# Key/value weight halves side by side in one stationary, and the norms' squares as the moving side of four column-tiled products

## The reference, cut to what matters

```python
qkv = einsum('bsd,ed->bse', x, Wqkv_w) + Wqkv_b        # 512 query columns, 32 key, 32 value
scores = einsum('bqhd,bkd->bhqk', q, k) / sqrt(32)     # causal
ctx = einsum('bhqk,bkd->bqhd', softmax(scores), v)
x = layernorm(x + ctx @ out_w.T + out_b)
top, sel = top_k(x @ router_w.T, 2)
h = silu(xb @ w1[sel]) * (xb @ w3[sel])                # bfloat16 products
x = layernorm(x + softmax(top) * (h @ w2[sel]))
```

## Time and profile before

| | |
|---|---|
| median of three runs | 1142.77 us |
| the profiled execution, device time | 1142.1 us |
| its span, first to last instruction | 1140.3 us |
| PE busy | 1085.1 us (95%) |
| DVE busy | 881.0 us (77%) |
| ACT busy | 715.3 us (63%) |
| POOL busy | 192.4 us (17%) |
| mean granted clock of TensorE | 0.985 |

### The profile page before, as it was taken

The page is one execution under the profiler, slowest core; times in us unless marked ns, Lnnn a source line. Parts: engine busy times, 40 slices in busy tenths (PEclk is TensorE's granted clock), DMA queues, the critical chain, the costliest instruction groups (busy, mean ns, idle before and its releaser), DMA issues.

```text
span 1140.3 us, 18344 instructions
## 1 busy us (share of the span) xinstructions
PE 1085.1 (95%) x6080; PEld 521.2 (46%) x6080; DVE 881.0 (77%) x1103; ACT 715.3 (63%) x844; POOL 192.4 (17%) x156
## 2 busy tenths in 40 slices
PE   6699999999999999999989999999999999999986
PEld 4246434743336543334734743474333654333442
DVE  3176799679985688988676669976998668898856
ACT  5344676558883488886436458744888437888721
POOL 2250223012112012111013013210211201211000
PEclk9799999999999999999999999999999999999988
DMA  4893430253001622000163254016400152200000
GB/s 139 220 168 77 117 74 9 72 126 92 1 1 39 149 75 38 1 1 18 46 153 86 65 121 112 2 40 146 112 1 1 39 119 68 38 1 1 2 1 37
DMA packets 41101, 74.36 MB, mean 65 GB/s; under 512 B 14224, under 2 KB 15248, under 8 KB 40976
## 3 DMA queue, kind: packets, MB, share of 16 engines
q1 hardware_dynamic: 25392, 58.74, 19.6%
q0 software_dynamic: 13584, 11.54, 6.8%
q10 hardware_dynamic: 2000, 2.51, 0.7%
HBM read 25.58 MB, written 8.39 MB: 30 GB/s over the span
## 4 chain that ended last, share of the span: by engine, by line
PE 83%; DVE 7%; issue 4%; ACT 2%; SPq 2%; POOL 2%; ACTq 0%; DMA 0%; DVEq 0%; POOLq 0%
PE sc L1109 22%; PE bank L1131 20%; PE sc L996 10%; PE sc L1249 9%; PE bank L996 7%; PE sc L1149 3%; DVE psum_k L793 3%; PE sc L1264 2%; SPq L393 2%; PE bank L1149 2%; PE bank L1264 2%; PE sc L1197 1%; PE bank L1257 1%; POOL prob L492 1%; ACT prob L620 1%
## 5 line engine op out<-in xcount | busy, mean ns | idle before, releaser
L620 ACT ACTIVATE prob<-sc 128x1024 f32<-128x1024 f32 x544 | 525.6, 1025 | 144.9 <-PE sc L1109 144.7
L793 DVE TENSOR_TENSOR psum_k<-psum_k,prob 128x2048 f32<-128x2048 f32 x170 | 403.5, 2373 | 4.7
L1109 PE MATMUL sc<-q_st,k_st 128*128 128x512 f32 x1088 | 329.4, 424 | 20.0 <-DMA q_st<-q_lo 8.7
L1109 PEld LDWEIGHTS sc<-q_st,k_st 128*128 128x128 f32 x1088 | 184.6, 189 | 262.9 <-ACT prob L620 177.7
L1131 PE MATMUL bank<-prob,v_sb 128*32 128x512 f32 x2176 | 287.4, 606 | 0.6 <-POOL prob L492 0.5
L492 POOL TENSOR_SCALAR_AFFINE_SELECT prob<-prob 128x1024 f32<-128x1024 f32 x64 | 112.2, 1793 | 539.8 <-ACT prob L620 539.8
L1249 PE MATMUL sc<-prob,w_sb 128*128 128x512 bf16 x512 | 120.8, 382 | 0.0
L1131 PEld LDWEIGHTS bank<-prob,v_sb 128*32 128x32 f32 x2176 | 44.4, 108 | 104.9 <-issue 87.4
L650 ACT ACTIVATE prob<-sc 128x512 f32<-128x512 f32 x64 | 38.0, 594 | 76.0 <-PE sc L1249 76.0
L996 PE MATMUL bank<-q_st,wq_hi 128*128 128x512 f32 x240 | 80.7, 401 | 0.0
L793 DVE TENSOR_TENSOR psum_k<-prob 128x2048 f32<-128x2048 f32 x28 | 64.0, 2287 | 19.8 <-POOL prob L492 15.8
(11 more groups left out here) (138 smaller groups left out, 996.0 us busy)
## 6 DMA issues: line engine op xcount, KB each, us to landing
q_st<-q_hi SPq DMA_DIRECT2D x128, 128.0 KB, 2.4
q_st<-q_lo SPq DMA_DIRECT2D x128, 128.0 KB, 2.4
res<-in_x SPq DMA_DIRECT2D x8, 1024.0 KB, 5.1
res<-ob_sb POOLq DMA_DIRECT2D x8, 1024.0 KB, 8.7
out_x<-res SPq DMA_DIRECT2D x32, 256.0 KB, 2.2
res<-in_xT SPq DMA_DIRECT2D x7, 1024.0 KB, 5.3
w_sb<-in_w POOLq DMA_DIRECT2D x8, 256.0 KB, 8.6
prob<-in_wqkvT ACTq DMA_DIRECT2D x4, 288.0 KB, 6.1
```

The source lines that it names most:

```text
L620: nc.scalar.activation(prob[t % NP][:, half * HW:(half + 1) * HW], score_half(q // TB, 2 * t + half).rearrange("p m n -> p (m n)"), ACT.Ex ...
L793: nc.vector.tensor_tensor(acc[:, :], first[:, :], prob[t % NP][:, :], ALU.add).then_inc(add_v, 1)
L1109: last = nc.tensor.matmul(dst, k_st[:, k * P:(k + 1) * P], q_st[slot][:, c * HJ:(c + 1) * HJ, at:at + P], start=True, stop=not shift)
```

## The change

The high halves of the key/value weights (64 columns) and their low halves (64 columns) stand side by side in `wq_hi`, so one product with 128 stationary columns gives high·high in rows 0 to 63 and low·high in rows 64 to 127 of the bank; a second one with 64 columns adds high·low to rows 0 to 63. ACT writes the lower 64 rows with the bias to `kv_sum`, DVE adds the upper 64 rows (`add_kv`), and keys, values and their squares are taken from `kv_sum`, which lies in SBUF. `split_low_k` moves behind the fourth residual. `turn_v` waits for DVE's addition instead of for ACT.

In `sum_squares` the selection matrices (now 32 columns wide) become the stationary side and the squares, 512 tokens at a time, the moving side; the result of head group j goes to rows 32j to 32j+31. A fifth product adds the keys' and values' squares (64 rows deep) to row 127. One maximum over 512 columns, one transpose, and a copy beside a maximum over 127 entries follow.

```diff
-        wq_hi = sb("wq_hi", [P, DC, D + 2 * HD], F32R)
-        wq_lo = sb("wq_lo", [P, DC, D + 2 * HD], F32R)
+        wq_hi = sb("wq_hi", [P, DC, D + 4 * HD], F32R)
+        wq_lo = sb("wq_lo", [P, DC, D], F32R)
...
             def split_high_k(b, g):
                 act.wait_ge(projected, count(b, projected, 5 * g + 1))
-                nc.scalar.activation(vT_sb[:, :], LOW[4][0:HD, :], ACT.Identity, bias=bvk_sb[0:HD, :])
+                nc.scalar.activation(kv_sum, LOW[4][0:2 * HD, :], ACT.Identity, bias=bvk_sb[:, :]).then_inc(kv_half, 1)
+                act.wait_ge(kv_ready, count(b, kv_ready, g + 1))
                 for part in (0, 2):
-                    last = nc.scalar.activation(k_st[...], LOW[4][HD:2 * HD, :], ACT.Identity, bias=...)
+                    last = nc.scalar.activation(k_st[...], kT_sb, ACT.Copy)
...
             def square_kv(b, g):
-                nc.scalar.activation(squares_kv[:, 0, :], vT_sb[:, :], ACT.Square)
-                nc.scalar.activation(squares_kv[:, 1, :], k_st[0:HD, cols].bitcast(F32), ACT.Square)
+                nc.scalar.activation(squares_kv, kv_sum, ACT.Square)
...
             for c in range(DC):
                 dve.wait_ge(first_high, 2 * c + 1)
-                nc.vector.tensor_tensor(wq_lo[:, c, :], wq_raw[c], wq_hi[:, c, :].bitcast(F32),
+                nc.vector.tensor_tensor(wq_hi[:, c, D + 2 * HD:D + 4 * HD], wq_raw[c][:, D:D + 2 * HD],
+                                        wq_hi[:, c, D:D + 2 * HD].bitcast(F32), ALU.subtract)
+                nc.vector.tensor_tensor(wq_lo[:, c, :], wq_raw[c][:, 0:D], wq_hi[:, c, 0:D].bitcast(F32),
...
+            def add_kv(b, g):
+                dve.wait_ge(kv_half, count(b, kv_half, g + 1))
+                nc.vector.tensor_tensor(kv_sum, LOW[4][2 * HD:4 * HD, :], kv_sum, ALU.add).then_inc(kv_ready, 1)
...
             def split_low_k(b, g):
                 for part in (1, 3):
-                    last = nc.vector.scalar_tensor_tensor(out=k_st[...], in0=LOW[4][HD:2 * HD, :], ...)
+                    last = nc.vector.tensor_tensor(k_st[...], kT_sb, k_st[0:HD, cols].bitcast(F32), ALU.subtract)
...
             def fold_norms(b, g):
-                nc.vector.reduce_max(norms[:, 0:1], src[:, 0:TB * H], AX)
-                nc.vector.reduce_max(norms[:, 1:2], src[:, TB * H:TB * (H + 1)], AX).then_inc(norms_ready, 1)
+                nc.vector.reduce_max(norms[:, :], squares_bank(g)[:, :], AX).then_inc(norms_ready, 1)
...
             def top_of_norms(b, g):
-                nc.vector.reduce_max(top_norms[0:1, :], top[1][0:1, 0:2 * P]..., AX).then_inc(top_ready, 1)
+                nc.vector.tensor_copy(top_norms[0:1, 1:2], top[1][0:1, P - 1:P])
+                nc.vector.reduce_max(top_norms[0:1, 0:1], top[1][0:1, 0:P - 1], AX).then_inc(top_ready, 1)
...
                     for t in range(TB):
                         if t == 3:
                             with if_more(dve, b, g):
-                                split_low_k(b, g + 1)
+                                add_kv(b, g + 1)
...
                     with if_more(dve, b, g):
+                        split_low_k(b, g + 1)
                         split_low_q(b, g + 1, 0)
...
+            def product_kv(c):
+                def high():
+                    return nc.tensor.matmul(LOW[4], wq_hi[:, c, D:D + 4 * HD], xT_hi[:, c, :],
+                                            start=(c == 0), stop=(c == DC - 1))
+                if c == 0:
+                    high()
+                last = nc.tensor.matmul(LOW[4][0:2 * HD, :], wq_hi[:, c, D:D + 2 * HD], xT_lo[:, c, :], ...)
+                return high() if c else last
...
             def turn_norms(b, g):
-                for n in range(2):
-                    last = nc.tensor.transpose(top[1][0:1, n * P:(n + 1) * P], norms[:, n:n + 1], ident[:, :])
+                nc.tensor.transpose(top[1][0:1, 0:P], norms[:, :], ident[:, :]).then_inc(norms_turned, 1)
...
             def sum_squares(b, g):
-                for t in range(TB):
-                    for j in range(HJ):
-                        nc.tensor.matmul(squares_bank(g)[:, at:at + HC], squares[:, j, toks], head_pick[:, :], ...)
-                    for n in range(2):
-                        last = nc.tensor.matmul(squares_bank(g)[:, ...], squares_kv[:, n, toks], ones_b[:, :], ...)
+                rows = [squares_bank(g)[j * HD:(j + 1) * HD, :] for j in range(HJ)]
+                for j in range(HJ):
+                    nc.tensor.matmul(rows[j], head_pick[:, :], squares[:, j, :], start=True, stop=(j < HJ - 1))
+                last = nc.tensor.matmul(rows[HJ - 1], kv_pick[:, :], squares_kv, start=False, stop=True)
```

More of the change, by code:

```diff
@@ L253, in build @@
         low_out = sem("low_out")
+        kv_half = sem("kv_half")
+        kv_ready = sem("kv_ready")
         vT_turned = sem("vT_turned")
@@ L316, in build @@
             stored[0]: 16 * TB * NG // 2, stored[1]: 16 * TB * NG // 2,
[L317 removed]
+            projected: 5 * NG, high_out: 5 * NG, low_out: 5 * NG, kv_half: NG, kv_ready: NG, vT_turned: NG, v_ready: NG,
             scored: 2 * NT, exped: 2 * NT, masked: 2 * NQ, pv_done: NT, add_v: ADDS,
@@ L700, in split_low_k @@
                 for part in (1, 3):
-                    last = nc.vector.scalar_tensor_tensor(
-                        out=k_st[part * HD:(part + 1) * HD, cols], in0=LOW[4][HD:2 * HD, :],
-                        scalar=bvk_sb[HD:2 * HD, :], in1=k_st[0:HD, cols].bitcast(F32),
-                        op0=ALU.add, op1=ALU.subtract)
+                    last = nc.vector.tensor_tensor(k_st[part * HD:(part + 1) * HD, cols], kT_sb,
+                                                   k_st[0:HD, cols].bitcast(F32), ALU.subtract)
                 last.then_inc(low_out, 1)
@@ L754, in judge @@
                                         ALU.mult).then_inc(verdict_ready, 1)
+            add_kv(0, 0)
             split_low_k(0, 0)
@@ L1003, in project_kv @@
                 for c in range(DC):
-                    last = product(LOW[4][0:2 * HD, :], (wq_hi, wq_lo), (xT_hi, xT_lo), c, slice(D, D + 2 * HD))
+                    last = product_kv(c)
                 last.then_inc(projected, 1)
@@ L1018, in turn_v @@
             def turn_v(b, g):
-                pe.wait_ge(high_out, count(b, high_out, 5 * g + 1))
+                pe.wait_ge(kv_ready, count(b, kv_ready, g + 1))
                 pe.sem_inc(waited_apart, 1)
@@ L1049, in _ @@
                 pe.wait_ge(first_low, 2 * (c + 1))
-                for bank, cols in ((LOW[4][0:2 * HD, :], slice(D, D + 2 * HD)), (q_bank(0, 0), slice(0, P))):
-                    last = product(bank, (wq_hi, wq_lo), (xT_hi, xT_lo), c, cols)
-                    if c == DC - 1:
-                        last.then_inc(projected, 1)
+                last = product_kv(c)
+                if c == DC - 1:
+                    last.then_inc(projected, 1)
+                last = product(q_bank(0, 0), (wq_hi, wq_lo), (xT_hi, xT_lo), c, slice(0, P))
+            last.then_inc(projected, 1)
             for j in range(1, HJ):
```

41 lines of the change are left out of this document (17 added, 24 removed).

## The result

| | before | after |
|---|---|---|
| median of four runs each | 1142.15 us | 1130.92 us |
| lowest and highest | 1138.89, 1143.15 | 1129.11, 1134.01 |
| profiled execution, device time | 1142.1 us | 1134.01 us |
| its span | 1140.3 us | 1132.2 us |
| mean granted clock | 0.985 | 0.984 |

The profiled execution of after is its slowest, 8.1 us faster than that of before. So the traces have to explain 8.1 us, and experiments the rest.

A forecast was written before the change was run, and what follows sets the result against it. A boundary was taken as bound by PE's queue of products. Seven at 0.91 + 0.49 − 0.21 = 1.19 us (8.3) plus 0.8 at the start-up made 9.1 us: 1133.0 profiled, 1133.7 median, range 1129.5 to 1139.

The forecast's parts named there:

- Key/value products: At each boundary: eight PE products remain of twelve; four fewer at 0.228 us each gain 0.91 us.
- Squares: At each boundary: five column-tiled products take 0.76 us in place of 1.25, a gain of 0.49, between +0.82 and −0.16.
- fixed part: In the squares: 0.13 us that remains fixed around column-tiled products, from rows of eight and twenty-four single-precision products.
- My entry of 0.10: In the squares: entering the column-tiled products costs 0.10 us, part of the 0.76.
- Gate transposes: DVE's longer maximum adds 0.37 us to the chain ending in `ghl`; PE starts them later, 0.21 us lost a boundary.
- Start-up: Before the first attention: four products go, less 0.08 us for DVE's subtraction; gain 0.83 us, SP's first transfer near 24.6.
- Seven copies within 0.3 us: The seven boundaries are copies of each other to within 0.3 us, so one near 897 us was worked out.
- my cover: Behind the key/value products: `normalise` ends 2.5 us before PE's transposes need it, so the new handover costs nothing.
- no overlap: Rival, squares: five products run one behind the other, 1.41 us; a boundary gains 0.54, total 1138.2 us; chance 0.12.
- drains: Rival, key/value products: each width switch drains the array, 0.23 us, six a boundary; 4.0 us slower, 1146.8; chance 0.05.
- DVE bounds the router: Rival, gates: the wide maximum runs at half the rate, +0.80 us; 2.9 us less gain, 1136.6; chance 0.10.
- taken back in attention: Rival: attention tied to SP's transfers, which begin only 0.91 us earlier, loses 0.28 us a boundary; 1135.7; chance 0.07.

The follow-up runs named there:

- one_path_after: After with attention's untaken second path (row maxima, shifted scores) left out of PE's and DVE's code; 1125.44 us, ratio 0.9859 to before.
- one_path_kv: After with the norms as before, and attention's untaken second path left out of PE's and DVE's code; 1129.58 us, ratio 0.9885 to before.
- squares_more: After with eight more products on squares ahead of the five: four on four column groups, then four on one; one run, 1143.29 us.
- warm: After with 24 products of a 128x128 identity on PE ahead of the first projection; 1136.18 us, ratio 0.9955 to before.
- add_late2: After with two more 64x512 additions on DVE, each waited for, ahead of `add_kv`; 1133.75 us, ratio 0.9929 to before.
- fold_early: After with the maximum of 512 columns moved from inside the router's chain to ahead of DVE's wait for the router's result; 1128.41 us, ratio 0.9897.
- norms_only: Before with only the new squares, one maximum and one transpose; keys and values computed as before; 1142.77 us over twelve runs, ratio 1.0017.
- one_path kernels: Kernels with attention's untaken second path left out of PE's and DVE's code; before so cut took 1136.70 us, after so cut 1125.44.

## Why the prediction was right, step by step

- **Key/value products: right.** 0.91 forecast; 0.88 at the last boundary (18.96 to 18.08), 6.43/7 = 0.92 over all, and without the second path 0.89 in one_path_after and 0.86 in one_path_kv. The fourth residual of after starts at 900.24, 4.83 us behind the first of them, where it was 908.60 − 902.03 = 6.57: 1.7 earlier, as forecast. Products with 128 and 64 columns alternate at 0.22 to 0.23 us, so a switch costs nothing. The Trainium skill, "TensorEngine Tiling (Array Packing)", Key Properties, has TensorE drained at a change of the tiling mode. For 128 against 64 columns this trace does not agree; for the entry to 32 columns it does, with 0.09 to 0.10 us.
- **Squares: right, in other parts, and from rows that did not carry it.** 0.49 forecast, (4.24 − 0.65)/7 = 0.51 measured. The five products take 0.65 + 0.09 for the entry = 0.74, where I had 0.76. By `squares_more`, the 0.33 us from the first four to the fifth has 0.23 for the four and so 0.10 for the change from 128 rows to 64, as assumed. The 0.32 from the fifth to the fold is its 0.216 and 0.10 more, where I had 0.13 as a fixed part. My entry of 0.10 lies ahead of the first product, not behind it. But the `x8` and `x24` of the earlier trace rows count instructions: the router's loop has four products, which leave eight. So the 0.43 us was the price of four such instructions, and did not show that four products run in the time of one. For bfloat16 this was assumed; `squares_more` bears it out.
- **Gate transposes: the sign right for DVE, the term mis-sized.** I had +0.21 a boundary; measured 0.43/7 = +0.06. Two things were missed. PE's own queue became shorter by 6.40 − 6.29 = 0.11 us when the second transpose of the norms fell away, which I had priced at nothing. And the chain from the copy of the router's result to `ghl` grew at this boundary from 930.95 − 926.07 = 4.88 to 923.06 − 918.06 = 5.00 us, by 0.12 and not 0.37: in before DVE stood 0.25 us in the middle of this chain, in after it does not there. Where it stands in neither kernel, at two boundaries, the chain grew from 4.60 to 5.00: 0.40, so the price of the maximum itself was right. The timeline of DVE in before:

```profile
926.07 0.19 DVE L914 COPY rsc<-bank 128x32 f32<-128x32 f32 x1 [0.83 <-PE bank L1240]
...
927.35 0.17 DVE L920 FIND_INDEX8 tidx<-top,rsc 128x8 uint32<-128x8 f32 x1 [0.25 <-issue]
```

  Such a gap moves from kernel to kernel, and inside one it stands at the same block of both sequences: at the two boundaries of after with 6.69 us DVE stands 0.64 us ahead of the maximum where it stands 0.29 at four others; `warm`, `add_late2` and `squares_more` have it at the same two. The maximum itself takes 0.69 us, where I had 0.65.
- **Start-up: failed.** I had −0.83 us and 24.6 us for SP's first transfer; it came at 25.77, +0.34 against the earlier trace rows. The four products fell away, but the others ran at PE's lower level for longer. The timeline of after:

```profile
7.96 0.80 PE L1010 MATMUL sc<-q_st,wq_hi 128*128 128x512 f32 x1 [7.96 <-DVE q_st L696]
...
12.81 0.63 PE L1010 MATMUL sc<-q_st,wq_hi 128*128 128x512 f32 x1
...
13.63 0.40 PE L1003 MATMUL bank<-q_st,wq_lo 128*128 128x512 f32 x1
...
25.77 1.22 SPq L396 DMA_DIRECT2D q_st<-q_hi  x2
```

  Products are 0.43 us apart until 13.63; in before until 11.26. The profile's clock column reads 1.00 in both, so here the level is to be read from the distances: 0.43 is twice 0.215, 1.2 GHz. Thirteen products fell at the lower level and not eight: 5 × 0.215 = 1.1 us, and the first one came 0.17 later. The first product with the short distance behind it starts between 10.9 and 11.9 us in the four traces with the old key/value products and between 12.0 and 13.7 in the seven with the new ones and no warm-up. That goes with the change, but the two sets all but touch, and the spread of 1.7 us inside the second says that an execution has a share in it; why the new order should delay the rise was not shown. Over these traces SP's first transfer lies at 25.3 to 25.8 us with the old products and at 25.1 to 25.9 with the new ones: nothing gained, and nothing lost that one trace could tell. The Trainium skill, "TensorE: Matmul & The Clock Gate", Part 1, says that the number of cold products (those at the lower level) at the start varies from run to run of the same kernel, and gives 6, 11 and 14. The traces here agree that it varies: `after`, `fold_early`, `add_late2`, `squares_more` and `one_path_after` have the same start-up, and 13, 12, 11, 10 and 9 such products.
- **"Seven copies within 0.3 us": wrong for DVE.** It holds for PE, whose stretches from the key/value products to the gate transposes repeat to 0.1 us in before (from there to attention the one between the sequences takes 19.98 us where the others take 11.9). DVE's residuals reach the handover to ACT 2.3 us later behind the second block of a sequence, where `add_late2` left at most 0.2 us of my cover. What waits first is PE's transposes of the values and its products behind DVE's `q_lo`, not the transposes of the normalised rows, by which I had worked out 2.5 us. Nothing was lost in after, by luck of size.
- **Not foreseen: the pauses.** The earlier trace rows had 4% issue in the chain, and I did not ask where. They made up most of +2.65 and −1.83 of the 8.1 us. Without the path that is jumped over, the pause ahead of the denominators is gone in four kernels of four, the kernel before is 0.5% faster, the norms' 3.4 us can be measured, and four to six runs of a kernel spread over 2.4 to 3.2 us where eleven to fifteen of before beside them spread over 5.4 to 5.7. That the pauses were what hid the norms' gain in `norms_only` is the likeliest reading; no trace of one of its longer runs was taken. That the engine's supply of instructions is late behind the jump is what I think; shown is that the pause goes with the skipped code.

The sum came out at 11.2 us between medians against 9.1, with some luck: the start-up's 0.83 us was not there, and the gates' term gave 7 × 0.25 = 1.7 us more than forecast. The profiled boundaries gave 10.0 us in the one_path kernels, 1.43 each (1.19 forecast): 0.24 more, nearly all of it the gates' term. The rest is pauses and the runs' spread. Of the rivals, "no overlap" and "drains" were shown false; "DVE bounds the router" is true as a wait, which the forecast had too, but its condition, half the rate, is not (0.69 us for 512 columns), and it cost 0.17 us a boundary and not 0.6; "taken back in attention" did not occur: the eight attentions differ by 0.89 us, of which 1.66 lie behind the changed pause.

## What to carry to other kernels

In a stretch where PE stands for under 1 us in 40, count the starts that go and multiply by the distance between starts; that term held to 3% here. Put a long operation into a gap of its engine's chain rather than between dependent small ones, and check what covers a handover at every repetition, on every engine, before calling repetitions copies. When an edit is worth less than the kernel's spread, look for waits on "issue" first, and measure the edit in a kernel that is free of them.

## What the runs showed of the hardware

- Four column-tiled bfloat16 products of 512 columns on four column groups start the next product after 0.23 us, four on one group after 0.86. Products for idle groups started at 376.08, ahead of two for a busy group that stand earlier in the program and started from 376.29 on (`squares_more`). Going from 128 to 64 rows of contraction costs 0.10 us; going between 128 and 64 stationary columns costs nothing (0.23 us between starts).
- PE can stand for 1 to 3 us with nothing to wait for behind a jump over a long untaken path, and, behind a pause of 2.97 us, run at 1.2 GHz (granted clock 0.50 from 75.00 to 78.40); behind one of 1.56 us it did not. That the jump is the reason is shown only so far as the pauses ahead of the denominators go when the skipped code is left out.
- After ten warming products and 1.90 us of standing, PE fell back to the lower level until some 12.3 us: that warm-up was lost.
- DVE's maximum over 128x512 from PE's banks takes 0.69 us, the same as an addition of 512 columns.
